# Sparse and windowed attention on one core: one score pass for local and compressed keys, and four smaller edits

## What is computed

```python
q  = apply_rope(rmsnorm(x @ Wq + bq, qn_w), pos)
ck = apply_rope(rmsnorm(entries @ Wk + bk, kn_w), block_ends)   # 256 keys
sc = where(causal, q @ ck.T * scale, NEG)
tv, ti = top_k(sc, 8)
e  = exp(tv - max(tv)) * (tv > NEG / 2)
ctx_sparse = (e / max(sum(e), 1e-9)) @ cv[ti]
sl = where(band, q @ window(lk).T * scale, NEG)                 # 128 before + 128 own
ctx_local = softmax(sl) @ window(lv)
out = x0 + ((ctx_sparse + ctx_local) / 2) @ Wo + bo + fp8_ffn(x)
```

## Time and profile before

| | us | share of the span |
|---|---|---|
| median of three runs | 2670.82 | |
| profiled execution, with launch and end | 2673.22 | |
| its span | 2671.4 | |
| TensorE busy | 2588.2 | 97% |
| VectorE busy | 2037.6 | 76% |
| ScalarE busy | 1678.9 | 63% |
| GpSimd busy | 1491.2 | 56% |

### The profile page before, as it was taken

How to read it: one execution, slowest core, us unless ns; L and a number is a source line. 1 busy time by engine, 2 the same in 40 slices (tenths; PEclk the granted TensorE clock), 3 DMA queues, 4 the chain that set the end, 5 groups by cost and what they waited for, 6 DMA issues and landing times. The chain is left out here.

```text
span 2671.4 us, 58405 instructions
## 1 busy us (share of the span) xinstructions
PE 2588.2 (97%) x16648; PEld 2316.3 (87%) x16648; DVE 2037.6 (76%) x7785; ACT 1678.9 (63%) x5845; POOL 1491.2 (56%) x2518
## 2 busy tenths in 40 slices
PE   3799999999999999999999999999999999999999
PEld 2688888888898888899988889889989999999998
DVE  5687888888878777787877777778777777777766
ACT  2556666666666666666666666666666666666665
POOL 3355555655567555556556656556555655555543
PEclk9899999999999999999999999999999999999999
DMA  3101111111231111111133111111113111111000
GB/s 108 41 29 45 49 48 41 33 56 41 68 115 53 49 44 50 47 45 45 52 108 96 37 45 45 45 49 52 45 57 114 56 33 33 37 33 33 29 17 33
DMA packets 150387, 137.06 MB, mean 51 GB/s; under 512 B 14258, under 2 KB 114100, under 8 KB 150068
## 3 DMA queue, kind: packets, MB, share of 16 engines
q1 hardware_dynamic: 150068, 133.33, 16.0%
HBM read 106.02 MB, written 27.26 MB: 50 GB/s over the span
## 5 line engine op out<-in xcount | busy, mean ns | idle before, releaser
L1198 POOL TENSOR_TENSOR t<-raw,tB 128x128 f32<-128x128 f32 x512 | 255.9, 519 | 683.5 <-DVE raw L820 683.2
L1168 POOL TENSOR_TENSOR r<-ss,mh 128x4 f32<-128x4 f32 x256 | 286.7, 1120 | 324.1 <-DVE ss L841 323.1
L452 PE MATMUL bQK<-wh,xh 128*128 128x512 f32 x1024 | 432.9, 423 | 0.0
L682 ACT ACTIVATE P<-P,nm,r 128x256 f32<-128x256 f32 (+1 forms) x512 | 301.1, 588 | 202.8 <-DVE nm L885 186.4
L676 ACT ACTIVATE raw<-raw,r 128x128 f32<-128x128 f32 x512 | 177.9, 395 | 369.9 <-POOL r L1168 314.9
L454 PE MATMUL bQK<-wh,xl 128*128 128x512 f32 x1024 | 404.9, 395 | 0.0
L453 PE MATMUL bQK<-wl,xh 128*128 128x512 f32 x1024 | 404.6, 395 | 0.0
L667 ACT ACTIVATE junk<-raw 128x128 bf16<-128x128 f32 x1024 | 305.9, 319 | 11.6 <-DVE raw L820 11.6
L470 PE MATMUL bVC<-wh,xl 128*128 128x256 f32 x1024 | 289.9, 283 | 0.0
L469 PE MATMUL bVC<-wl,xh 128*128 128x256 f32 x1024 | 289.5, 283 | 0.0
L468 PE MATMUL bVC<-wh,xh 128*128 128x256 f32 x1024 | 289.3, 282 | 0.0
(11 more groups left out here) (156 smaller groups left out, 7590.2 us busy)
## 6 DMA issues: line engine op xcount, KB each, us to landing
wr<-in_Wq SPq DMA_DIRECT2D x128, 128.0 KB, 2.4
wr<-in_Wlk SPq DMA_DIRECT2D x128, 128.0 KB, 2.7
wr<-in_Wlv SPq DMA_DIRECT2D x64, 256.0 KB, 3.1
wr<-in_Wo SPq DMA_DIRECT2D x64, 256.0 KB, 2.6
out<-acc SPq DMA_DIRECT2D x32, 256.0 KB, 2.9
ini<-in_hidden_states SPq DMA_DIRECT2D x24, 256.0 KB, 3.1
xs<-xsh SPq DMA_DIRECT2D x24, 256.0 KB, 2.0
xs<-xsl SPq DMA_DIRECT2D x24, 256.0 KB, 2.6
```

The costliest lines, as they stand in the source:

```text
L452: e.matmul(bQK[:, :], a, b, start=kt == 0, stop=False)
L682: e.activation(pl, pl, ACT.Exp, scale=r4[:, u % 4, 2 * h:2 * h + 1], bias=nm[:, u % 4, h, 1:2], accum_out=su[:, u % 4, h, 1:2]).then_inc(S ...
L1168: e.tensor_tensor(r4[:, u % 4], ss[:, u % 4], mh[:, 0:4], ALU.pow).then_inc(S["r4"], 1)
L1198: last = e.tensor_tensor(t2[:, :, :, d_], raw[:, u % 2, :, :, s_], tB[:, :, u % 8, d_].unsqueeze(1).broadcast_to([128, 2, 2, 32]), ALU.mult)
```

## The change

One score pass: qkh and qkl become one row per head of five slots of 128: query, two key slots used in turn (by u % 2), and 256 compressed keys. For each head three fp32r matmuls of 256 + C columns give all scores; qf and ckf go. In tile 0 the other key slot is computed and not read. Between batches GpSimd copies the new compressed keys into the slots (new_ck). The query has one slot only, so hi_qk waits for the scores of the unit before.

The output product and add_out move to lag 5, and out_proj stands ahead of turn_p. Squares become one operation over 512 elements; VectorE sums them (sum_qk). The top 8: neg_max handles both heads in one operation; ScalarE exponentiates the eight maxima (exp_8) and all scores (exp_s); strike takes the eight exponentials out of the exponentials (match_replace to 0), and GpSimd subtracts the rest from the whole (keep_8), which leaves the eight; sum_8 sums the eight. rope_rest goes to GpSimd. The loops of VectorE, ScalarE and GpSimd are reordered, tile stages from tile 8 on get one more step, and chunk positions move.

```diff
-FIRST, LAST = -AHEAD, NU + 5
+FIRST, LAST = -AHEAD, NU + 6
...
-LAGS = {"stats": 0, "power": 0, "norm": 1, "turn": 1, "hi": 1, "max": 2, "ew": 2, "lo": 2, "wm": 3, "et": 3,
-        "park": 3}
+LAGS = {"stats": (0, 0), "power": (0, 0), "norm": (1, 1), "turn": (1, 2), "hi": (1, 2), "max": (2, 3), "ew": (2, 3),
+        "lo": (2, 3), "wm": (3, 4), "et": (3, 4), "park": (3, 4)}
...
-                e.matmul(loc, q_, kh, start=True, stop=False)
-                e.matmul(loc, q_, kl, start=False, stop=False)
-                e.matmul(loc, ql_, kh, start=False, stop=True)
-                if i < 4:
-                    e.matmul(cmp, qf[:, u % 2, h, :], ckf[:, b % 2, 0:C], start=True, stop=True).then_inc(S["s"], 1)
-                    return
-                e.matmul(cmp, q_, ckh[:, b % 2, 0:C], start=True, stop=False)
-                e.matmul(cmp, q_, ckl[:, b % 2, 0:C], start=False, stop=False)
-                e.matmul(cmp, ql_, ckh[:, b % 2, 0:C], start=False, stop=True).then_inc(S["s"], 1)
+                n = 256 + C
+                q_, ql_ = qkh[:, h, 0, :], qkl[:, h, 0, :]
+                kh = qkh[:, h, 1:5, :].rearrange("p a c -> p (a c)")[:, 0:n]
+                kl = qkl[:, h, 1:5, :].rearrange("p a c -> p (a c)")[:, 0:n]
+                e.matmul(bS[h][:, 0:n], q_, kh, start=True, stop=False)
+                e.matmul(bS[h][:, 0:n], q_, kl, start=False, stop=False)
+                e.matmul(bS[h][:, 0:n], ql_, kh, start=False, stop=True).then_inc(S["s"], 1)
...
                 if u1 is not None:
                     tr(u1)
+                if u5 is not None:
+                    out_proj(u5, 0)
+                    out_proj(u5, 1)
                 if u3 is not None:
                     turn_p(u3, 0)
                     turn_p(u3, 1)
-                if u4 is not None:
-                    out_proj(u4, 0)
-                    out_proj(u4, 1)
...
-                for k in range(4):
-                    last = e.activation(junk[:, k, :], raw[:, u % 2, k // 2, k % 2, :], ACT.Square,
-                                        accum_out=ss[:, u % 4, k:k + 1])
-                last.then_inc(S["sq"], 1)
+                    e.wait_ge(S["sqs"], u)
+                e.activation(pair(sq[:, :, :]), flat(raw[:, u % 2]), ACT.Square).then_inc(S["sq"], 1)
...
+                e.activation(e8[:, u % 2, h, :], mm[:, u % 4, h, 0:8], ACT.Exp, scale=r4[:, u % 4, 2 * h:2 * h + 1],
+                             bias=nm[:, u % 4, h, 0:1]).then_inc(S["e8"], 1)
...
+                e.tensor_reduce(ss[:, u % 4], sq[:, :, :], mybir.AxisListType.X, ALU.add).then_inc(S["sqs"], 1)
...
-                e.match_replace(rp[:, h, 0:C], mm[:, u % 4, h, 0:8], bS[h][:, 256:256 + C], GONE).then_inc(S["mr"], 1)
-
-            def pick(u, h):
-                C = width(u)
-                e.wait_ge(S["es"], 2 * u + h + 1)
-                if u >= 2:
-                    e.wait_ge(S["pt"], 2 * (u - 2) + h + 1)
-                e.scalar_tensor_tensor(out=P[:, u % 2, h, 256:256 + C], in0=rp[:, h, 0:C], scalar=GONE,
-                                       in1=es[:, h, 0:C], op0=ALU.is_equal, op1=ALU.mult,
-                                       accum_out=su[:, u % 4, h, 0:1]).then_inc(S["stt"], 1)
+                e.wait_ge(S["e8"], a + 1)
+                e.wait_ge(S["es"], a + 1)
+                if u >= 1:
+                    e.wait_ge(S["sub"], u)
+                e.match_replace(rp[:, h, 0:C], e8[:, u % 2, h, :], es[:, u % 2, h, 0:C], 0.0).then_inc(S["mr"], 1)
+
+            def sum_8(u):
...
+            def rope_rest(u):
...
+            def keep_8(u):
+
+                C = width(u)
+                e.wait_ge(S["mr"], 2 * u + 2)
+                if u >= 2:
+                    e.wait_ge(S["pt"], 2 * (u - 2) + 2)
+                e.tensor_tensor(P[:, u % 2, :, 256:256 + C], es[:, u % 2, :, 0:C], rp[:, :, 0:C],
+                                ALU.subtract).then_inc(S["sub"], 1)
```

More of the change, by code:

```diff
@@ L425, in run_sync @@
                     load_ini(t)
+            for u in range(NU - 7, NU):
+                store(u)
             for i in range(NT):
@@ L608, in run_tensor @@
             for s in range(FIRST, LAST):
-                u0, u1, u2, u3, u4 = (unit_at(s, lag) for lag in range(5))
+                u0, u1, u2, u3, u4, u5 = (unit_at(s, lag) for lag in range(6))
                 if u0 is not None:
@@ L773, in run_scalar @@
                     kscale(u1)
-                if u2 is not None:
-                    exp_l(u2, 0)
                 if u4 is not None:
@@ L778, in run_scalar @@
                 if u2 is not None:
+                    exp_8(u2, 0)
+                    exp_8(u2, 1)
                     exp_s(u2, 0)
+                    exp_s(u2, 1)
                 if u1 is not None:
                     hi_qk(u1)
+                if u0 is not None:
+                    squares(u0)
                 if u3 is not None:
@@ L784, in run_scalar @@
                     put_p(u3, 1)
-                for q, c in enumerate(CHUNKS):
-                    if c[0] == "o" and c[3] == s:
-                        hi_wo(q)
-                if u2 is not None:
-                    exp_s(u2, 1)
-                if u0 is not None:
-                    squares(u0)
-                if u2 is not None:
-                    exp_l(u2, 1)
+                if u1 is not None:
+                    put_v(u1)
                 if tile_at(s, "hi") is not None:
@@ L799, in run_scalar @@
                     cast_x(tile_at(s, "hi"))
-                if u1 is not None:
-                    put_v(u1)
+                if u2 is not None:
+                    exp_l(u2, 0)
+                    exp_l(u2, 1)
+                for q, c in enumerate(CHUNKS):
+                    if c[0] == "o" and c[3] == s:
+                        hi_wo(q)
                 if tile_at(s, "ew") is not None:
@@ L1020, in init @@
                 if t < 8:
-                    done = [u for u in range(t, 64, 8) if u < s - 4]
+                    done = [u for u in range(t, 64, 8) if u < s - 5]
                     if done:
@@ L1086, in run_vector @@
                 if u1 is not None:
+                    sum_qk(u1)
                     eps_qk(u1)
                     rope_a(u1)
-                if u3 is not None and u3 % 8 == 0:
-                    sums(u3)
-                if tile_at(s, "stats") is not None:
-                    norm_stats(tile_at(s, "stats"))
+                if tile_at(s, "lo") is not None:
+                    lo_x(tile_at(s, "lo"))
                 if u1 is not None:
@@ L1124, in run_vector @@
                 if u2 is not None:
-                    neg_max(u2, 1)
-                    pick(u2, 0)
-                    strike(u2, 1)
+                    strike(u2, 0)
                 if u1 is not None:
                     lo_qk(u1)
-                if u4 is not None:
-                    add_out(u4)
+                if u2 is not None:
+                    strike(u2, 1)
+                    sum_8(u2)
+                if ffn_at(s, 3) is not None:
+                    init(ffn_at(s, 3), s)
+                if u5 is not None:
+                    add_out(u5)
+                if tile_at(s, "stats") is not None:
+                    norm_stats(tile_at(s, "stats"))
+                if tile_at(s, "norm") is not None:
+                    normalise(tile_at(s, "norm"))
                 if block_at(s, "rope") is not None:
@@ L1138, in run_vector @@
                     neg_r(u1)
-                if u2 is not None:
-                    pick(u2, 1)
-                if u0 is not None:
-                    rope_rest(u0)
                 if ffn_at(s, 0) is not None:
@@ L1235, in run_gpsimd @@
                 u0, u2 = unit_at(s, 0), unit_at(s, 2)
+                if u2 is not None and u2 % 64 == 63 and u2 + 1 < NU:
+                    new_ck(u2 // 64 + 1, 0)
                 if u0 is not None:
                     rope_b(u0)
+                    rope_rest(u0)
+                if u2 is not None and u2 % 64 == 63 and u2 + 1 < NU:
+                    new_ck(u2 // 64 + 1, 1)
                 if ffn_at(s, 2) is not None:
```

240 lines of the change are left out of this document (132 added, 108 removed), and 2 rows, old and new, of the table SIGNALS.

## The result

The changed kernel takes 2766.89 us (median of four runs, 2763.88 to 2772.51), the kernel before 2671.8 beside it (2670.68 to 2673.38). The ratio is 1.0358, with a 95% interval from 1.0339 to 1.0377. Forecast were 2610 us and a range up to 2644; 157 us lie between forecast and result, on the side that the prediction gave 0.05.

What follows compares the result with a forecast made beforehand. TensorE's instruction issue was taken as the bound. The terms -38 + 4 - 14 + 1 - 7 - 11 + 4 gave -61 us, so the median would become 2610 us, range 2592 to 2644.

Steps and rivals of the forecast that it cites:

- What bounds the kernel: TensorE instruction issue: the unvarying 76.18 us group period is no wait, so a matmul removed is time removed.
- One score pass, -38: Scores on TensorE: six matmuls of 256 + C columns per unit save 1.19 us a group, 32 groups, -38 us.
- The straight line between 256 and 512 columns: Score matmul price at widths between 256 and 512 columns: linear from 0.119 to 0.232 us.
- Output product one step later, +4 and -14: TensorE order: one more plain fp32 to fp32r change per step, +4 us; the wait for cl at L539 goes, -14.
- The price of the order: TensorE's extra change from plain fp32 to fp32r: 0.015 us a step, 256 steps, +4 us.
- VectorE by arrival, -7 and -11: VectorE reordered: norm_stats, normalise and init at step end; kscale waits -7 us, startup -11.
- The startup term: First x tiles and steps: weights4 ahead of norm_stats -5 us, lo_qk ahead of normalise -6, together -11.
- The -7: Loader waits at L478 for kscale and transposes, 14.1 us: half saved by moving norm_stats to VectorE's step end.
- a sign that it would be wrong: TensorE waiting at the successors of L478 or L511 for kscale or normalise_p would show the forecast wrong.
- The small operations, +4 for what was not seen: Small VectorE, ScalarE and GpSimd operations, GpSimd about 7.2 of 9.5 us a step; trouble in x-tile steps +4 us.
- The cover of normalise_p: GpSimd, plain step: normalise_p ends near 4.2 us, and turn_p behind the output product needs it at 7.8.
- the one slower rival: Score matmuls wider than 256 columns cost what 512 cost: +38 instead of -38, ending at 2686 us; chance 0.05.

Runs made afterwards that it cites:

- e4_split: Kernel with both repairs, local and compressed keys scored in separate matmuls again (tiles 0 to 3: compressed high halves only, plain fp32): 2645.11 us, 0.990 of before.
- e1_init: Changed kernel with init on VectorE back right after neg_max, ahead of lo_c: 2646.4 us, 0.9908 of before.
- both repairs: Changed kernel with two edits, init back after neg_max and hi_wo back after put_p: 2602.72 us, 0.9739 of before.
- e2_hiwo: Changed kernel with hi_wo on ScalarE back after put_p, ahead of put_v: 2716.68 us, 1.017 of before.
- e5_outlate: Kernel with both repairs, output product behind the P transposes again on TensorE, still at lag 5: 2618.17 us, 0.9797 of before.
- e9_both_sum: Kernel with both repairs, sum_qk and eps_qk moved to VectorE's previous step, behind add_out: 2593.77 us, 0.9713 of before.
- e6_before_init_late: Kernel before the change, with only init moved from ahead of lo_c to behind lo_qk on VectorE: 2736.91 us, 1.0244 of before.

## Why the prediction was wrong, point by point

**What bounds the kernel.** Right: with the stops gone, TensorE's instructions decide again, and a matmul taken away is time taken away (e4_split's 42.4 us). But one step of the reading does not hold. The prediction says that a period that never varies is instruction issue and not a wait. In the kernel after, the last batch comes back every 76.06 us just as regularly, and each group holds a stop of 1.23 us.

**One score pass, -38.** Right. By the score blocks of the last batch, start to start, 9.93 us a group became 8.70: 1.23 us (forecast 1.19). By the group period with e4_split it is 1.49 (76.28 to 74.79), by the run 42.4 us. The difference lies in the blocks of the values, which stand behind the scores: 11.45 us a group with the pass split, 11.21 with one pass. The straight line between 256 and 512 columns held: widest unit 1.37 us for six, 0.228 each. The 131 ns at 512 columns that the Trainium skill gives ("TensorE: Matmul & The Clock Gate", "Back-to-back issue gap") is not shown by any fp32r matmul here.

**Output product one step later, +4 and -14.** The price of the order was right (0.01 us a step). The wait for cl is gone. But the part says of L539 only that it "will now find ch and cl a step old". It has a third input, its bank, which ffn fills and init frees. **This is where the working failed**: the operation was moved ahead of eight transposes, and only two of the three things that it waits for were looked up. The row to look for was not among those of waits, since before it never waited; it had to be read from the code.

**VectorE by arrival, -7 and -11.** The second half of the same failure: "It moves to the end of the step, and so do normalise and init." norm_stats and normalise were priced, init was not, though each moved step must be asked who waits for it. Price: 120.5 us in e1_init, of which some 87 are the wait and some 35 the lower clock after it. The startup term held: first scores 5.4 us earlier, first group 88.1 us instead of 104.2. The -7 did not come: with both repairs the loader still waits 14.5 us for kscale (14.1 before). The prediction counted half of this wait as gained, with excess and rejoin ahead of sum_qk as the reason why not all; none of it was gained. With sum_qk moved ahead of that work the wait falls to 7.0 us and the run by 9.

**hi_wo and lo_wo.** The section on the change lists both at their new places, and the prediction prices neither: "The weight split goes behind normalise_p" is about another one. Price: 50.2 us in e2_hiwo. The prediction had the parts of the chain in its own working: it put kscale at 2.8 us and its need at 5.9, a cover of 3.1. That number rests on ScalarE and VectorE being free at the step's start. In the step shown above, half 0 begins at 2329.49 and lo_wo ends only at 2333.08. sum_qk, eps_qk, power_qk and kscale need 2.8 us from there (2333.00 to 2335.82), so kscale is done 6.3 us into the step, not 2.8, and nothing is left of the 3.1. The prediction had named TensorE waiting for kscale as a sign that it would be wrong, and this is the sign that came: 60.9 us at L480.

**The small operations, +4 for what was not seen.** Near. keep_8 measured 799 ns on the mean over its eight widths, 318 for the narrowest to 1276 for the widest, within the bounds 0.52 and 1.32 but for the two narrowest (318 and 456). VectorE's reduction took 0.679 against 0.69. GpSimd stands at 1766.5 us; 7.2 of 9.5 us a step were forecast, 1766.5 by 256 is 6.9. The cover of normalise_p (3.6 us by a plain step) is overrated: without the output product in front, 53 loads wait for it in e5_outlate.

```profile
L844 DVE TENSOR_REDUCE ss<-sq 128x4 f32<-128x512 f32 x256 | 173.8, 679 | 0.0
...
L1197 POOL TENSOR_TENSOR P<-es,rp 128x512 f32<-128x512 f32 x32 | 40.8, 1276 | 2.3 <-DVE rp L902 2.3
```

(Both from the kernel with both repairs, grouped by line and shape: busy us, mean ns.)

**The sum and the rivals.** -61 was forecast for the terms listed; with the two stops removed the chip gave -69. The sum was incomplete, and that it comes so near without the stops is in part luck. The first group, up to the ninth unit's scores, ends 22 us earlier (165.7 instead of 187.6) where the start was given 11. All that comes later gained 49 in the profiled executions where 50 were forecast, although the -7 came to nothing. No rival was the mechanism that came true: the one slower rival was a price of matmuls, and nothing in it was about order. A list of moved steps, each with its releaser and its waiter, would have given this rival.

**Open.** Why the clock fell after most of the long stops and not after the others is not shown. In e9_both_sum some 7 us of waits at the transposes are left and not traced.

## What to carry to other kernels

When an engine's order is rewritten, list every call that changes place and write beside each who frees what it writes and who waits for what it frees; PSUM banks that two products share are part of that list, although no wait shows in the trace before. A copy or an addition that frees a bank costs nothing where it stands early, and here some 2.8 us of TensorE, 32 times, where it stands behind an operation that itself waits for the end of the step. Look at what stands behind a cross-engine hand-over at the step's end (here hi_wo to lo_wo): everything at the start of the next step inherits its delay.

## What the runs showed of the hardware

TensorE's granted clock dropped to the lower level after many of the stops in an otherwise full stream: 0.43 us for 512 columns behind such a stop, 0.23 elsewhere. Of 38 stops of 2.6 us and more between 190 and 2600 us in the kernel after, 25 had a stretch at that level behind them and 13 had none. So a stop can cost more than its length: 120.5 us were won where some 87 were waited. The stops of 1.95 us of e6_before_init_late cost 65 us for 62.4.

A VectorE operation can be held until one on GpSimd ends, and not only when it has two tensor inputs. wm, a 32-element operation with one tensor and a column from SBUF, took 256 ns on the mean before and 562 after (200 to 2600 us). With two subtractions in a row on GpSimd it was caught more often (837):

```profile
L1021 DVE TENSOR_SCALAR wm<-cst,smt 128x32 f32<-128x32 f32 x23 | 12.9, 562 | 0.8
...
L1022 DVE TENSOR_SCALAR wm<-cst,smt 128x32 f32<-128x32 f32 x23 | 19.2, 837 | 0.8
```

The first line is of the kernel after, the second of the one with the subtraction twice. In that kernel's timelines:

```profile
230.58 1.07 DVE L1022 TENSOR_SCALAR wm<-cst,smt 128x32 f32<-128x32 f32 x1
```

```profile
230.61 1.00 POOL L1200 TENSOR_TENSOR scr<-es,rp 128x384 f32<-128x384 f32 x1
```

Both end at 231.6. VectorE's operation, 0.24 us long where GpSimd is idle, lasts as long as the one on GpSimd. In the kernel with the subtraction twice, 18 of the 32 wm last until the added subtraction (L1200) ends, to within 0.05 us. The section that the prediction named (the Trainium skill, "SBUF — State Buffer", the shared port pair) names VectorE operations with two SBUF inputs, and those in a 2-port perf mode. wm has one tensor input; whether it runs in such a mode no run here shows.

For rope_add, which has two SBUF inputs, the prediction feared that the new load would hold it. The opposite came: 499 ns on the mean before, 426 after (200 to 2600 us). In the kernel before, 30 of 256 took 0.71 to 1.41 us, each beside the split of a weight chunk on GpSimd:

```profile
1482.17 1.41 DVE L846 TENSOR_TENSOR raw<-t 128x256 f32<-128x256 f32 x1
```

```profile
1481.88 1.41 POOL L1211 TENSOR_TENSOR wl<-wr,wh 128x512 fp32r<-128x512 f32 x1
```

In the kernel after it runs beside power_qk, which does not hold it, and 3 of 256 took longer than 0.5 us.
